# A graph-network kernel: its edge loop, its general path and its last stage put into one block, and its early sums kept on chip

## What is computed

```python
x = _layernorm(x + _L0_gnn_ref(x, edge_index, 6250))     # degree-normed sum over neighbours
# _L1: for every edge
gate = silu(edge_attr @ W1.T + b1) @ W2.T + b2 + adapt_logit
msg  = gate * h[dst] * (cw * mj)[:, None]
agg  = segment_sum(msg, src, N) / clip(segment_sum(mj, src, N), 1e-8)
x = _layernorm(x + _layernorm(h + agg) * gamma + beta)
```

## Time and profile before

| What | Time |
|---|---|
| Median of 3 runs | 3051.34 us |
| The three runs | 3043.43, 3051.34, 3051.47 us |
| The profiled execution | 3027.21 us |
| Its span, first to last instruction | 3025.4 us |
| DVE busy | 2404.3 us (79%) |
| PE busy | 2250.1 us (74%) |
| POOL busy | 2121.9 us (70%) |
| ACT busy | 1395.5 us (46%) |

### The profile page before, as it was taken

One profiled execution on the slowest core, in us unless ns is written; L12 is line 12 of the kernel. 1 busy time (PEld: TensorE's weight loads), 2 busy tenths in 40 slices (PEclk: granted clock), 3 DMA queues, 4 the chain that ended last, 5 costly groups with the idle time before them and its releaser, 6 DMA issues. The chain is left out here.

```text
span 3025.4 us, 73628 instructions
## 1 busy us (share of the span) xinstructions
PE 2250.1 (74%) x25909; PEld 1913.9 (63%) x25909; DVE 2404.3 (79%) x5424; ACT 1395.5 (46%) x2929; POOL 2121.9 (70%) x1852
## 2 busy tenths in 40 slices
PE   6980476678777787777787877787878787788475
PEld 5760365566666666655666666676767666667475
DVE  9994577777787777877788897888888878887698
ACT  7982244444444444444444444444444444445123
POOL 7506777877777777777777777777777777760165
PEclk9765688888888888988888898888989888979797
DMA  8405233333433434333344454444444444442896
GB/s 322 148 2 163 62 112 108 101 126 116 127 113 115 127 115 124 117 112 112 118 148 153 143 155 146 147 145 145 145 147 147 144 144 145 156 138 103 333 389 224
DMA packets 174987, 441.53 MB, mean 146 GB/s; under 512 B 92662, under 2 KB 92662, under 8 KB 154806
## 3 DMA queue, kind: packets, MB, share of 16 engines
q1 hardware_dynamic: 103754, 236.05, 23.4%
q0 software_dynamic: 67888, 194.98, 20.7%
q10 hardware_dynamic: 3004, 5.90, 0.6%
HBM read 292.51 MB, written 144.27 MB: 144 GB/s over the span
## 5 line engine op out<-in xcount | busy, mean ns | idle before, releaser
L722 POOL DMA_INDIRECT slot<-table,gidx x1616 | 1811.9, 1121 | 633.6 <-issue 620.2
L821 PEld LDWEIGHTS route<-parts,oh_r 128*128 128x128 bf16 x11312 | 764.9, 100 | 91.6 <-issue 66.9
L821 PE MATMUL route<-parts,oh_r 128*128 128x148 bf16 x11312 | 812.9, 232 | 3.2 <-DVE parts L1224 3.0
L1089 DVE TENSOR_SCALAR oh_r<-iota_r,spot 128x896 bf16<-128x896 f16 x1616 | 613.5, 451 | 74.4 <-PE route L821 74.4
L894 ACT ACTIVATE routed<-route 128x444 bf16<-128x444 f32 (+1 forms) x1010 | 507.9, 513 | 258.5 <-PE route L821 240.0
L856 PE MATMUL pwin<-slot,oh_d 128*128 128x144 bf16 x1616 | 167.6, 276 | 404.2 <-DMA slot<-table,gidx 372.1
L856 PEld LDWEIGHTS pwin<-slot,oh_d 128*128 128x128 bf16 x1616 | 147.8, 155 | 428.2 <-issue 270.0
L777 PEld LDWEIGHTS pwin<-win,oh_t 128*128 128x128 bf16 x4848 | 262.3, 117 | 200.6 <-issue 101.8
L777 PE MATMUL pwin<-win,oh_t 128*128 128x80 bf16 (+1 forms) x4848 | 277.0, 227 | 77.1 <-ACT ssum L904 71.6
L747 PE MATMUL phid<-attr,w 80*96 80x512 f32 x404 | 282.2, 789 | 44.4 <-issue 44.1
L1195 DVE TENSOR_TENSOR prod<-slot,got 128x256 f32<-128x256 f32 x202 | 84.6, 419 | 231.3 <-ACT parts L955 231.2
(11 more groups left out here) (228 smaller groups left out, 3257.3 us busy)
## 6 DMA issues: line engine op xcount, KB each, us to landing
rows<-slots SPq DMA_DIRECT2D x51, 1295.0 KB, 8.8
oh_t<-dst_row SPq DMA_DIRECT2D x101, 512.0 KB
erows<-slots SPq DMA_DIRECT2D x51, 777.0 KB
attr<-in_edge_attr SPq DMA_DIRECT2D x101, 320.0 KB
slots<-zeros SPq DMA_DIRECT2D x53, 518.0 KB
slot<-table,gidx POOLq DMA_INDIRECT x1616
table<-tab SPq DMA_DIRECT2D x3, 676.0 KB, 5.9
weight_t<-weights SPq DMA_DIRECT2D x101, 8.0 KB
```

What stands on the lines that cost most here:

```text
L722: e.indirect_dma_start(out=slot[:, s, g, :], out_offset=None, in_=table0, in_offset=bass.IndirectOffsetOnAxis(ap=gidx[:, s, g:g + 1], axis ...
L821: mm = e.matmul(route[:, (NPH * m + phase) % 2, RC * (j - a):RC * (j - a + 1)], oh_r[:, c, slot_of, :], parts[:, s % 2, c, :], start=(c == ...
L1089: oh = e.tensor_scalar(oh_r[:, c], iota_r[:, :, :], spot[:, s % 2, c:c + 1], None, ALU.is_equal)
```

## The change

The three blocks behind the setup become one. The five programs of each former block are now functions (`sync`, `gpsimd`, `tensor`, `scalar`, `vector`) that are told how to go on: the loop's program ends, still inside `when(e, 1)`, with the last stage's program for data that fit; the general path's program ends, inside its `when(e, 0)`, with a second copy of the last stage's program. Buffers of the three parts still share the same places in SBUF and PSUM, semaphores no longer do. In place of the meeting of all engines, SP, POOL and DVE each wait, at the start of the last stage, for all scatters to have landed; POOL's wait at the end of the loop is gone.

`early_sums`, `epart`, `early`, `early_out` and `eout` are gone: DVE writes each early sum to its place in `agg`, which now lives through the whole program, and POOL adds the late sum to it in place. `count` is filled by three bf16 copies from `number` (the same numbers, each 16 times over) in place of the cast.

The diff without changes of indentation and of semaphore scopes, and without the general path's own waits:

```diff
@@ loop
+        scattered = [sem(f"scattered{s}") for s in range(2)]
+        weights_out = sem("weights_out")
+        def tile_programs(ph):
...
-                    def early_out(i, s):
-                        if not visits(i, s):
-                            return
-                        e.wait_ge(emade, 2 * visit(i, s) + 2)
-                        e.dma_start(early_sums[:, bass.ds(visited(i, s) * MW, MW)], epart[:, :]).then_inc(eout, 16)
...
-                                   (early_out, 7, EARLY_FROM), (early_rows, 5, EARLY_FROM))
-                        e.wait_ge(eout, 16 * NB)
+                               (early_rows, 5, EARLY_FROM))
+                    go_on(e)
...
                     over_tiles(e, NT, U, (gather, 0), (scatter, 6))
-                        for s in range(2):
-                            e.wait_ge(scattered[s], 16 * ((NT - s + 1) // 2))
+                    go_on(e)
...
                     e.wait_ge(ecopied, 2 * v + 2)
-                        if not isinstance(v, int) or v > 0:
-                            wait_apart(e, eout, 16 * v, passed)
-                        e.tensor_reduce(epart[:, :], ethree[:, :].rearrange("p (k c) -> p c k", c=MW), AX.X, ALU.add
+                    e.tensor_reduce(agg[:, bass.ds(visited(i, s), 1), :].rearrange("p o c -> p (o c)"),
+                                    ethree[:, :].rearrange("p (k c) -> p c k", c=MW), AX.X, ALU.add
                                     ).then_inc(emade, 1)
@@ last stage, for data that fit
+            def sync(e, fits):
+                if fits:
+                    for parity in range(2):
+                        e.wait_ge(scattered[parity], 16 * ((NT - parity + 1) // 2))
                     for b in range(NB):
...
-                            if b == 0:
-                                e.dma_start(early[:, :, :].rearrange("p b c -> p (b c)"), early_sums
-                                            ).then_inc(early_in_stored, 16)
-                                stores[0] += 1
...
+            def gpsimd(e, fits):
+                if fits:
+                    for parity in range(2):
+                        e.wait_ge(scattered[parity], 16 * ((NT - parity + 1) // 2))
                 e.memset(expo[:, :], -0.5).then_inc(shifted, 1)
...
-                        e.tensor_tensor(agg[:, b, :], most[:, b % 2, :], early[:, b, :], ALU.add).then_inc(added, 1)
+                    e.tensor_tensor(agg[:, b, :], agg[:, b, :], most[:, b % 2, :], ALU.add).then_inc(added, 1)
...
-                        done(e.tensor_copy(count[:, :, :], bc_last(iota_f[:, :], COLS)))
+                    for parity in range(2):
+                        e.wait_ge(scattered[parity], 16 * ((NT - parity + 1) // 2))
+                    for a in range(0, COLS, G):
+                        n = min(G, COLS - a)
+                        done(e.tensor_copy(count[:, :, a:a + n], number[:, :, 0:n]))
@@ one block
+        with ExitStack() as ph:
+            tiles = tile_programs(ph)
+        with ExitStack() as ph:
+            far = far_programs(ph)
+        with ExitStack() as ph:
+            last = last_programs(ph)
+            with nc.Block() as block:
+                @block.sync
+                def _(e):
+                    tiles.sync(e, lambda e: last.sync(e, True))
+                    far.sync(e, lambda e: last.sync(e, False))
...
```

More of the change, by code:

```diff
@@ L1 @@
+from collections import namedtuple
 from contextlib import ExitStack, contextmanager
@@ L63 @@
 DEEP = 2048
+Programs = namedtuple("Programs", "sync gpsimd tensor scalar vector")
 def bc_mid(ap, n):
@@ new lines, in tensor @@
+            def tensor(e, fits):
+                if fits:
+                    for b in range(NB):
+                        e.wait_ge(rows_in[b % RS], 16 * (b // RS + 1))
+                        e.wait_ge(ohs, b + 1)
+                        if b >= 2:
+                            e.wait_ge(summed, b - 1)
+                        for c in range(COLS):
+                            mm = e.matmul(acc[:, b % 2, 0:3 * MW], onehot[:, b % OS, :, c],
+                                          rows[:, b % RS, c, 0:3 * MW], start=(c == 0), stop=(c == COLS - 1))
+                        mm.then_inc(used, 1)
@@ L1579, in _ @@
-                    with when(e, 1):
-                        for b in range(TURNS):
-                            if b < NB:
-                                e.wait_ge(rows_in[b % RS], 16 * (b // RS + 1))
-                                if b >= OS:
-                                    e.wait_ge(ohs, b - OS + 1)
-                                e.activation(mine[:, b % OS], rows[:, b % RS, :, RC - 1], ACT.Copy
-                                             ).then_inc(keyed, 1)
-                            if 2 <= b <= NB + 1:
-                                put(b - 2)
-                            beside(b, (square(0), 4), (scale(0, normal), 8), (square(1), 11), (scale(1, ready), 15))
@@ L1590, in _ @@
-                    with when(e, 0):
-                        in_waves(square(0), scale(0, normal), square(1), scale(1, ready))
+                    tiles.scalar(e, lambda e: last.scalar(e, True))
+                    far.scalar(e, lambda e: last.scalar(e, False))
+                @block.tensor
+                def _(e):
+                    tiles.tensor(e, lambda e: last.tensor(e, True))
+                    far.tensor(e, lambda e: last.tensor(e, False))
+                @block.gpsimd
+                def _(e):
+                    tiles.gpsimd(e, lambda e: last.gpsimd(e, True))
+                    far.gpsimd(e, lambda e: last.gpsimd(e, False))
@@ L1683, in _ @@
-                @block.tensor
-                def _(e):
-                    with when(e, 1):
-                        for b in range(NB):
-                            e.wait_ge(rows_in[b % RS], 16 * (b // RS + 1))
-                            e.wait_ge(ohs, b + 1)
-                            if b >= 2:
-                                e.wait_ge(summed, b - 1)
-                            for c in range(COLS):
-                                mm = e.matmul(acc[:, b % 2, 0:3 * MW], onehot[:, b % OS, :, c],
-                                              rows[:, b % RS, c, 0:3 * MW], start=(c == 0), stop=(c == COLS - 1))
-                            mm.then_inc(used, 1)
+                    tiles.vector(e, lambda e: last.vector(e, True))
@@ L1697 @@
+                    far.vector(e, lambda e: last.vector(e, False))
 def kernel(**inputs):
```

1721 lines of the change are left out of this document (866 added, 855 removed).

## The result

The kernel after took 3026.0 us (median of 5 runs, 3017.23 to 3029.43), the kernel before 3043.43 us in the comparison (5 runs, 3036.94 to 3051.47): ratio 0.9932, 95% interval 0.9905 to 0.9958. That is faster by 0.7%, inside the range of 3020 to 3050. By the ratio the difference is 20.7 us (interval 12.8 to 28.9), by the medians 17.4; the sum said 15.4. The profiled execution took 3017.23 us with a span of 3015.4, 10.0 us less than the one of before.

The account below looks back on a forecast made before the run. POOL bounds the loop, pure waiting the gap after it, loads and then DVE the last stage. -13.1 - 3.0 + 0 + 0.7 = -15.4 us, from the median 3051.34 to 3036 us; range 3020 to 3050.

Parts of the forecast that it names:

- Step 1: Gap between loop and last stage: SP issues the first rows load once the last scatter lands, 13.1 us gained.
- Rival D: Gap between loop and last stage doesn't close, the scatter truly needing the drain's 7.6 us: 3043 us, chance 0.04.
- Step 2: Start of last stage: without the early_sums load DVE starts its bound part 3.0 us sooner; loop's stores worth 0.
- Step 3: Start of last stage: filling count by three bf16 copies, taken as 2.6 us, at worst 7.9, is worth 0.
- The first one-hot directly behind its keys: Sign at the start of the last stage: DVE's first one-hot follows the keys of bucket 0 without delay.
- Step 4: Kernel's end: POOL's only drain after the loop now comes last, 0.7 us lost; SP's longer branches taken as 0.
- A: Loop's second half: more gathers meet DVE's one-hots, 4.7 us each, making the kernel slower, 3067 to 3083 us; chance 0.07.
- B: Loop takes back most gain through two to four slow gathers, or last stage gains less: 3042 to 3047; chance 0.15.
- C: Loop gains too, by at most 9.7 us of index-load waits or fewer long gathers, 4.7 each: 3027 us; chance 0.16.
- The span from the first gather to the last scatter: Sign in the loop: the prediction is wrong if this span moves by more than 5 us.
- The last stage was to be 207.4 us: Sign: from first load to last instruction, about 206.7 us plus 0.7 instead of 209.7.

Follow-up runs that it names:

- the third comparison: On one chip beside before (3033.51 us): early sums on chip alone, ratio 0.9993; one block alone, 0.9962; the whole change, 0.9953.
- the early drain: Kernel after with POOL's x_bet addition waiting for the count copies and a POOL drain right behind that addition: 3015.32 us, ratio 0.9917.
- the two-block kernel: Kernel after with the loop in its own block, ended by POOL's scatter wait, general path and last stage in a second: 3021.1 us, ratio 0.9938.
- the second comparison: Four variants of after (load kept, two blocks, x_bet behind count, that plus early POOL drain): 3020.59, 3021.1, 3022.41, 3015.32 us, beside before's 3038.82.
- the two halves: Before with early sums kept on chip, three blocks: ratio 0.9993; after with early sums through HBM again, one block: 0.9962.

## Why the prediction was right

**What bounds the kernel: right.** Both the gap and the DMA-bound start of the last stage were what the change shortened, and behind them DVE stayed the bound.

**Step 1, -13.1: right, in size and place.** The gap shrank by 13.1 us in the pair of profiles and by 13.2 to 13.3 in the third comparison. Rival D (the drain is time that the scatter needs) is out: with the drain gone the first load is still 4.7 us behind the last scatter, at its landing. SP's wait costs next to nothing more. The split that step 1 left open is known now: the drain and the first meeting 8.8, the second block 4.4, of which 3.2 is the time in which only PE and DVE were missing.

**Step 2, -3.0: right in mechanism, and in size within what the runs spread over.** In three blocks it is worth 2.2 to 2.4 us (209.89 to 207.72, 209.71 to 207.35). In one block it is 2.9 to 3.6 (210.53 to 207.66, 211.15 to 207.56), and a load of that size put back costs 2.8. Keys of bucket 12 come 2.2 us sooner in the first pair. In that pair DVE gives some of the 3.0 away in short waits (5.1 us left, not 4.2). The 3.6 is more than the bound of 3.0 by bytes; 0.1 of it lies behind the last output's issue, the rest wasn't traced. That the loop's 51 stores and waits are worth nothing behind POOL holds to the accuracy of the ratio: 0.9993 (0.9978 to 1.0007) with the last stage's 2.2 us in it.

**Step 3, 0: right, for the reason given; the size and one sign were off.** The copies took 7.09 us, near the worst case, and 2.06 when free; my 2.6 was a fair length without `x_bet`. "The first one-hot directly behind its keys" was wrong: it was 1.5 us late, where before it was 1.3. It cost nothing: the second one-hot began 0.8 us behind its keys, the third 0.3, and DVE was waiting for keys again. The Trainium skill (SBUF — State Buffer, SBUF: two separate sides) has the rule of whole instructions shutting each other out, and this case agrees with it in three arrangements: copy behind `x_bet` 5.75 us instead of 0.76, cast ahead of it 2.51 with `x_bet` at 7.57, and neither disturbed when one waits for the other.

**Step 4, +0.7: right in size, partly wrong in cause.** From the last output's issue to the end it is 3.31 us instead of 2.70, +0.6. POOL's drain ends only 0.2 us behind SP's and the early drain won 0.4; in after the remaining 0.3 lies between SP's last issue and its drain, and it is there too in the two-block kernel and in the three-block one without the early load. It isn't a price of the longer branch: in the one-block kernel with sums in HBM SP's drain comes 2.54 us behind its last issue, before 2.48. It goes with the early load: SP's drain comes 2.80 to 2.83 us behind its last issue in every kernel without that load and 2.47 to 2.54 in every one with it. It isn't the transfer, since the kernel with a load of that size put back has 2.84. What it is stays open. SP's branches took at most 45 ns, while one of PE's took 3616. So the rule of the Trainium skill (Runtime: NRT & Kernel Launch, Instruction fetch mechanics), by which SP might have paid, asked nothing of SP here:

```profile
L563 SPq COMPARE_BRANCH  x3: 38/40/45, 240.9 to 3014.5; - x3
...
L563 PEldq COMPARE_BRANCH  x2: 82/1849/3616, 247.9 to 2989.5; - x2
```

PE's is at 2989.5, with 25 us of other engines' work behind it. Before, PE's long branch lay in the gap, where the meeting waited for PE and DVE; that is part of what step 1 gained.

**The rivals.** A and B lived on more gathers that meet DVE's one-hots. They didn't come: 8 gathers took over 4 us in before and 8 in after, 8 or 9 in every other kernel at this loop speed. C, a gain of the loop, was what the first result looked like (20.7 us off, 3026.0), and the second comparison, with 16.4 to 23.5 us by the medians (the expectation of before again names 17.7 as the lowest, wrongly), made it look likelier. The third comparison has 14.3 us for the same kernel, 8.5 to 20.3 by its interval, which leaves out C's 24.8 (one long gather fewer, 20.1, it just takes in); the two halves add up without it, and neither of C's two places, the index loads and the long gathers, shows a gain.

So the time below 3036 in the first result has no step of the change behind it that I could show. For the larger part the base had moved: before's median was 3051.34 in the three runs that I started from and 3043.43 over five, and 3043.43 - 15.4 is 3028.0, 2.0 above the result. That 3026.0 stands so near C's 3027 is chance, and there was some luck in that it lies inside the range: the base had moved by 7.9 us, and 6 were to spare.

For the second comparison, the two-block kernel's 12 us beyond its stages stay open: of before there is no profile on that chip, and a chance of the runs, or a loop of before that is longer on that chip alone, both fit.

**The signs.** The span from the first gather to the last scatter was to move by no more than 5 us. It moved by +3.3 and -1.7 us in the two pairs of before and after, but by +21.4 us between before and the kernel with the sums on chip, whose time didn't rise by the ratio (0.9993). This sign was too narrow for single profiles. The last stage was to be 207.4 us and is 208.1 and 207.6.

## What to carry to other kernels

When blocks follow each other, look first at what the engines' meeting waits for: here it was GpSimd's drain of 7.6 us behind indirect DMAs, 8.8 us with the meeting, while the data were ready, and then PE and DVE, PE with a branch of 3.45 us over a program that wasn't run. The drain can be moved to where nothing waits for GpSimd, PE's branch to where PE's work is done. A removed load is worth its transfer time only as far as the next bound has waits to give. A difference of 5 us in a loop of 2400 that varies by over 20 from one execution to the next can't be read from two profiles: run the halves beside the whole and see whether they add up, and set each profile against its own kernel's median.

## What the runs showed of the hardware

POOL's first drain behind the loop's indirect DMAs takes 7.58 to 7.71 us whether it stands 5 or 205 us behind the last of them, and any later drain 0.1 to 0.2 us. So it is not waiting for a transfer. Behind the setup block's 51 indirect DMAs POOL's drain takes 4.23 us in before (from 123.6 us, the last of them issued at 120.3); what sets the length wasn't tried.

A DVE copy or cast and POOL's addition of 128x2448 f32 exclude each other, and in these traces the one that starts first goes first, instruction by instruction. One cast of 2.5 us that begins first costs POOL 2.2 us; the same fill cut into three copies gives POOL its turn behind the first copy, and costs DVE 5.0 us. Cutting an instruction can cost more than it saves, when the other engine stands ready.

One chip did the same loop in 3570.7 us instead of 2398.0. Two of the long waits from 1400 to 2600 us there, the kernel after:

```profile
POOL slots L726 <- ACT routed L888: 227.1, 16, 18.1
PE route L815 <- issue: 220.6, 193, 9.9
```

The gathers are no slower (1067 ns there, 1129 here in that stretch), but POOL stands idle for 620 us of the 1200, against 270 here: 227 us behind ACT's `routed`, 73 behind its index loads, 63 behind PE, and the rest with no wait that the profile shows. PE, too, stops for up to 9.9 us with nothing to wait for that the profile shows. PE's route matmuls took 265 ns at the granted clock of 0.73 and 229 at 0.88; 36 ns more for each of 3696 of them is 133 us of the 1200. Which of these stops comes first, and what is behind them, wasn't tried; the loops of all four kernels profiled there are alike in length.
